# From the second write into the feed-forward: where the first units, the sums and the drain stand in each engine's queue

## The chip, the cores and the metric

The kernel runs on one core of one Trainium2 chip. The metric is the device time of one execution in microseconds; lower is better. The five engines of the core take their instructions in program order, each from its own queue, and wait for each other on semaphores. They are called PE (TensorE, matmuls), DVE (VectorE), ACT (ScalarE), POOL (GpSimd) and SP (SyncE, which issues the DMAs here).

## The reference, cut to what matters

The input x has 2 x 1024 rows of 2048 values. A block of attention and MLP is added to it, and then a feed-forward with quantised weights. The second write ends the first part, the feed-forward is the second:

```python
        out = o_d[..., :H]                       # y @ wod.T, and the low part of the deltas
        delta = jax.nn.softplus(delta_low @ du_w.T + du_b)
        A_neg = -jax.nn.softplus(A_logit)
        A_bar = jnp.exp(delta * A_neg)
        B_bar = (A_bar - 1.0) / (A_neg - SSM_EPS) * B_proj
        return (hs * A_full + out * B_full).reshape(b, l, H * C)
...
    x = x + _L0_xattn_ref(_layernorm(x, axis=-1), ...)
    x = x + _L0_ffn_ref(_layernorm(x, axis=-1), ...)   # w = (q - zp) * scale; out = x @ w.T + bias
```

## The kernel before

The last part of the program is one block (`build_middle`) in which `w1`, `mlp`, `w2` and `ffn` follow each other on every engine. The two that matter are the second write, `w2`, and the feed-forward, `ffn`. There are 16 tiles of 128 rows (`TILES`).

**The second write.** `steps` runs a software pipeline. In step s, tile s is loaded and split (`live(0)`), the products of tile s - 1 run on PE (`live(1)`, L1731: 48 triples of products, float32 done as high and low parts), tile s - 2 gets its gates, softplus and deltas (`live(2)`), tile s - 3 is updated and stored to the tensor x3 (`live(3)`, `res`), tile s - 4 is normalised and turned on PE (L1763), and tile s - 5 is stored turned, to xnT. The last five or six steps (s = 16 to 21) only empty the pipeline. After each of them `steps` calls `after(s - 16)`, and that is where the feed-forward puts its first work ahead: `sync_ahead`, `tensor_ahead`, `scalar_ahead`, `vector_ahead`. In step 17 (tile 15 in `live(2)`, nothing in `live(1)`) PE does `turn_small` (L1742) and `deltas` (L1748); ACT needs the first for `dlT` (L1871) and the second for the softplus (L1831 to L1837), which DVE's gates (L1976 to L1982) and POOL's gains (L1918 to L1926) wait for.

**The feed-forward.** 64 units: the 2048 outputs are four planes of 512 (c = u // 16), each over the 16 tiles. A unit is 16 x 3 matmuls of 128x512 (L2492 to L2494) into one of two banks `psF`. Its rows come from xnT into `xl` (`load_x`, three buffers, 1 MB), ACT copies the high part to `xh` (`hi_x`, L2383, two buffers), and DVE subtracts it to leave the low part (`lo_x`, L2387). The sum x3 comes into `xb` (`load_base`, two buffers, 256 KB), POOL adds the bias (L2475), DVE adds the bank (`finish`, L2448), SP stores it to y. The weights of plane 0 lie ready in the tensor wF: eight pairs are loaded (`load_first`, 512 KB each) and split by ACT (L2392) and DVE (L2397). Those of plane c + 1 are made during tiles 4 to 11 of plane c, two pieces to a unit (`made_in`): SP loads them (`load_piece`, 256 KB each, and every second unit two tiles of scales and zeros, `sz`, whose access repeats each of 8 rows 16 times), DVE subtracts the zeros (`less_zero`, L2416), POOL multiplies (L2421), ACT copies the high part (L2404), DVE leaves the low part (L2409).

What sets the order is the text itself. DVE's queue for unit u is

```python
                for v in made_in(u):
                    less_zero(dve, v)
                finish(dve, u)
                if u + 2 < UNITS:
                    lo_x(dve, u + 2)
                for v in made_in(u):
                    lo_piece(dve, v)
```

PE's unit u waits for `x_lo` of its own rows and `y_ok` of unit u - 2. `load_x(u)` waits until the buffer is free, `mm_ok >= u - 2`, which is the end of unit u - 3; the four first ones wait for the turned tile's store as well.

## Time and profile before

| | us |
|---|---|
| median of three runs | 2422.25 (2421.19 to 2428.3) |
| the profiled execution | 2416.85 |
| its span, first to last instruction | 2415.1 |
| PE busy in the span | 2188.6 (91%) |
| PE's weight loads | 1794.0 (74%) |
| DVE, ACT, POOL busy | 1329.1 (55%), 1068.7 (44%), 982.2 (41%) |

Times in the profile are us from the start of the span, of one execution. A row of a timeline gives start, duration, engine, line and operation with what it writes and reads, and in brackets how long its engine stood idle before it and what released it. The span lies 1.75 us under the execution's own time, and that 5.4 us under the median. The last matmul of the second write ends at 1637.1; the feed-forward's 64 units start between 1657.3 and the end.

### The profile page before, as it was taken

How to read it: one execution, taken by the hardware profiler on the slowest of the kernel's cores; microseconds unless marked ns; L12 is line 12 of the kernel's file. 1: busy time of each engine (PE TensorE's matmuls, PEld its weight loads, DVE VectorE, ACT ScalarE, POOL GpSimd, SP SyncE). 2: the span in 40 equal slices, each digit the busy share in tenths (PEclk: the TensorE clock that was granted, in tenths of full speed). 3: DMA queues.
4: the chain of work that ended last, by engine and by line, in shares of the span. 5: the costliest groups of instructions: out<-in, count | busy, mean ns of one | idle time of the engine just before them, and what ended most of it. 6: DMA issues, size and time to landing. Idle time of an engine off the chain costs nothing.

```text
span 2415.1 us, 34037 instructions
## 1 busy us (share of the span) xinstructions
PE 2188.6 (91%) x11560; PEld 1794.0 (74%) x11560; DVE 1329.1 (55%) x1744; ACT 1068.7 (44%) x1595; POOL 982.2 (41%) x613
## 2 busy tenths in 40 slices
PE   4898958999994999799999999995599999999999
PEld 2777745666663888688788889994478888888887
DVE  4777745777754899423332267675256265265222
ACT  2445425888882788621322356654222122122111
POOL 0111115999994777300000287762144144154110
PEclk8899987999996999899999999997799999999999
DMA  3678741333324666445454567866365465465443
GB/s 130 199 246 247 241 142 58 101 98 101 98 63 153 209 239 240 163 135 170 153 156 147 182 260 296 306 250 252 121 218 192 140 200 192 159 198 192 139 149 96
DMA packets 208614, 424.61 MB, mean 176 GB/s; under 512 B 16434, under 2 KB 131890, under 8 KB 181636
## 3 DMA queue, kind: packets, MB, share of 16 engines
q1 hardware_dynamic: 208516, 423.31, 53.3%
q8 instruction: 61, 1.00, 0.2%
q14 instruction: 37, 0.30, 0.0%
HBM read 284.31 MB, written 138.67 MB: 175 GB/s over the span
## 4 chain that ended last, share of the span: by engine, by line
PE 57%; DVE 4%; ACT 3%; DMA 2%; issue 2%; POOL 1%; SPq 0%; DVEq 0%; ACTq 0%; POOLq 0%
PE s_psF L2492 10%; PE s_psF L2493 10%; PE s_psF L2494 10%; PE s_m_psG L2141 7%; PE s_m_psU L2141 7%; PE s_w_psA L1731 4%; PE s_w_psB L1731 4%; PE s_w_psT L1763 1%; DVE s_w_ab L1511 1%; PE s_w_psB L1202 1%; DMA s_f_xl<-xnT 1%; PE s_w_psR L1250 1%; PE s_w_psT L1748 1%; PE s_w_psA L1212 1%; PE s_w_psT L1233 0%
## 5 line engine op out<-in xcount | busy, mean ns | idle before, releaser
L2492 PE MATMUL s_psF<-s_f_wh,s_f_xh 128*128 128x512 f32 x1024 | 402.7, 393 | 52.6 <-DVE s_f_xl L2387 32.3
L2494 PE MATMUL s_psF<-s_f_wh,s_f_xl 128*128 128x512 f32 x1024 | 401.3, 392 | 0.0
L967 POOL TENSOR_TENSOR s_a_pl<-s_a_pf,s_a_ph 128x1024 fp32r<-128x1024 f32 x128 | 302.0, 2391 | 22.2 <-ACT s_a_pf L932 22.1
L2383 ACT ACTIVATE s_f_xh<-s_f_xl 128x2048 fp32r<-128x2048 f32 x64 | 122.8, 1918 | 391.7 <-PE s_psF L2494 347.6
L2492 PEld LDWEIGHTS s_psF<-s_f_wh,s_f_xh 128*128 128x128 f32 x1024 | 194.4, 190 | 94.3 <-DVE s_f_xl L2387 33.1
L877 DVE TENSOR_REDUCE s_a_mx<-s_psS 128x1 f32<-128x512 f32 (+7 forms) x256 | 185.0, 754 | 119.5 <-PE s_psS L807 119.1
L2475 POOL TENSOR_TENSOR s_f_xb<-s_f_xb,s_f_fb 128x512 f32<-128x512 f32 x64 | 94.2, 1473 | 353.1 <-DMA s_f_xb<-x 353.1
L1895 POOL TENSOR_TENSOR s_w_yl<-s_w_y,s_w_yh 128x1024 fp32r<-128x1024 f32 x32 | 76.1, 2404 | 372.1 <-ACT s_w_yh L1809 372.1
L2494 PEld LDWEIGHTS s_psF<-s_f_wh,s_f_xl 128*128 128x128 f32 x1024 | 194.3, 190 | 40.7
L2493 PE MATMUL s_psF<-s_f_wl,s_f_xh 128*128 128x512 f32 x512 | 202.4, 395 | 0.0
L2387 DVE TENSOR_TENSOR s_f_xl<-s_f_xl,s_f_xh 128x2048 fp32r<-128x2048 f32 x64 | 160.9, 2514 | 71.5 <-ACT s_f_xh L2383 71.5
L2448 DVE TENSOR_TENSOR s_f_xb<-s_psF,s_f_xb 128x512 f32<-128x512 f32 x64 | 44.0, 687 | 250.7 <-PE s_psF L2494 218.1
L929 ACT ACTIVATE s_a_ph<-s_psX 128x1024 fp32r<-128x1024 f32 (+1 forms) x160 | 150.8, 942 | 57.0 <-PE s_psX L833 53.3
L2421 POOL TENSOR_TENSOR s_f_q<-s_f_q,s_f_sz 128x512 f32<-128x512 f32 x48 | 116.0, 2436 | 140.0 <-DVE s_f_q L2416 140.0
L458 POOL TENSOR_TENSOR s_q_qk<-s_q_ra,s_q_rb 128x1024 f32<-128x1024 f32 x16 | 37.7, 2359 | 294.8 <-DVE s_q_rb L690 294.8
L799 PE MATMUL s_psS<-s_a_k,s_a_q 96*128 96x512 f32 (+3 forms) x384 | 124.4, 413 | 35.4 <-DVE s_a_mx L877 19.7
L2493 PE MATMUL s_psF<-s_f_wl1a,s_f_xh 128*128 128x512 f32 x384 | 149.4, 389 | 0.0
L2201 DVE TENSOR_TENSOR s_m_mo<-s_m_psU,s_m_sil 128x512 f32<-128x512 f32 x64 | 44.2, 690 | 176.9 <-PE s_m_psU L2141 109.3
L851 PE MATMUL s_psO<-s_a_ph,s_a_vs 128*65 128x512 f32 (+3 forms) x384 | 128.5, 351 | 7.4 <-POOL s_a_pl L967 7.4
L932 ACT ACTIVATE s_a_pf<-s_psX 128x1024 f32<-128x1024 f32 x128 | 131.0, 1024 | 0.0
L851 PE MATMUL s_psO<-s_a_pl,s_a_vs 128*65 128x512 f32 (+3 forms) x384 | 125.3, 338 | 0.0
L2493 PEld LDWEIGHTS s_psF<-s_f_wl,s_f_xh 128*128 128x128 f32 x512 | 98.4, 192 | 20.5
(311 smaller groups left out, 5583.6 us busy)
## 6 DMA issues: line engine op xcount, KB each, us to landing
s_f_xl<-xnT SPq DMA_DIRECT2D x64, 1024.0 KB, 5.6
s_q_xt<-xT SPq DMA_DIRECT2D x16, 1024.0 KB, 7.7
s_q_xc<-xP SPq DMA_DIRECT2D x16, 1024.0 KB, 9.7
hsD<-s_q_hs SPq DMA_DIRECT2D x16, 1024.0 KB, 4.9
s_w_hin<-hsD SPq DMA_DIRECT2D x16, 1024.0 KB, 4.9
hs<-s_w_res SPq DMA_DIRECT2D x16, 1024.0 KB, 3.9
s_m_raw<-giT SPq DMA_DIRECT2D x32, 512.0 KB, 4.6
mlpT<-s_m_mo SPq DMA_DIRECT2D x64, 256.0 KB, 2.4
```

The lines of the kernel that those rows point to most:

```text
L799: pe.matmul(psS[:, at:at + n], qa[0:K3, p, qi * P:(qi + 1) * P], ka[0:K3, p, kk:kk + n], start=True, stop=not last)
L851: mm = pe.matmul(psO[0:VW, half, 512 - n:512], vs[:, r, ki, :], part[:, r, at:at + n], start=(ki == 0 and part is ph), stop=(ki == (3, 7)[ ...
L877: dve.tensor_reduce(mx[:, slot % 2, qi:qi + 1], psS[:, off:off + (qi + 1) * P], AX, ALU.max).then_inc(mx_ok, 1)
L929: act.activation(ph[:, r, at:at + wide[j]], src, ACT.Exp, scale=scale).then_inc(exp_ok, 1)
L932: act.activation(full, src, ACT.Exp, scale=scale).then_inc(exp_ok, 1)
L967: pool.tensor_tensor(pl[:, r, cols], pf[:, j - 1], ph[:, r, cols], ALU.subtract).then_inc(pl_ok, 1)
L1731: mm = pe.matmul(bank[:, 0:n], a[:, p, kt], b[:, kt, cols], start=False, stop=(kt == KM - 1 and a is yl))
L2141: mm = pe.matmul(bank[u % 2][:], a[:, kt], b[:, :, kt], start=(i == 0 and a is w[m][0] and b is xh), stop=(i == KH - 1 and a is w[m][1]))
L2387: dve.tensor_tensor(xl[u % 3][:], xl[u % 3][:].bitcast(F32), xh[:, u % 2], ALU.subtract).then_inc(x_lo, 1)
L2492: pe.matmul(out[:], xh[:, u % 2, kt], high(c, kt), start=(kt == 0), stop=False)
L2493: pe.matmul(out[:], xh[:, u % 2, kt], low(c, kt), start=False, stop=False)
L2494: mm = pe.matmul(out[:], xl[u % 3][:, kt], high(c, kt), start=False, stop=(kt == KD - 1))
```

## The change

Nothing is computed differently; instructions and DMAs move within the queues, and with them the waits.

- PE: units 0 and 1 move from behind step 16 into step 17 (`amid`), behind `turn_small` and `deltas`.
- ACT: behind step 16 only `hi_x(0)` remains. The eight copies of the first weights, `hi_x(1)` and `hi_x(2)` move into step 17, behind `dlT` and ahead of the softplus. `hi_x(3)` and `hi_x(4)` follow steps 17 and 18.
- DVE: `finish(0)` and `lo_x(2)` stand in step 17 behind the gates, ahead of the statistics; `finish(1)`, `lo_x(3)` behind step 17, `finish(2)`, `lo_x(4)` behind step 18.
- POOL: the first two sums are copied (with the bias) behind steps 16 and 17.
- SP: tile 0's rows are loaded behind step 16 once the products of tile 14 are done; the rest follows step 17. `serve(u)` (store of y, load of the sum u + 2, load of the rows u + 4) runs for units 0 to 2 between the last steps, the wait for all of the write's stores (`drained`) only then, and `serve` for units 3 to 63 in the loop. Before, the loop loaded the rows u + 3, ahead of the sum.

```diff
         def sync_ahead(sp, i):
             if i == 0:
+                sp.wait_ge(w2["ab_mm"], 2 * (TILES - 1))
+                load_x(sp, 0)
+            if i == 1:
                 sp.wait_ge(w2["ab_mm"], 2 * TILES)
-                load_x(sp, 0)
                 for pair in range(PAIRS):
                     load_first(sp, pair)
                 load_x(sp, 1)
-            if i == 1:
+                load_base(sp, 0)
                 sp.dma_start(fb[:], io["fbias"]).then_inc(fb_in, 16)
-                load_base(sp, 0)
                 load_base(sp, 1)
                 load_x(sp, 2)
-            if i == 2:
                 load_x(sp, 3)
+            if 2 <= i < 5:
+                serve(sp, i - 2)
+
+        def serve(sp, u):
+
+            c, tile = u // TILES, u % TILES
+            sp.wait_ge(y_ok, u + 1)
+            sp.dma_start(io["y"][tile * P:(tile + 1) * P, c * H:(c + 1) * H], xb[:, u % 2]).then_inc(y_out[u % 2], 16)
+            if u + 2 < UNITS:
+                load_base(sp, u + 2)
+            if u + 4 < UNITS:
+                load_x(sp, u + 4)
 
         def sync(sp):
-            for u in range(UNITS):
+            w2["drained"](sp)
+            for u in range(3, UNITS):
                 c, tile = u // TILES, u % TILES
                 if FROM <= tile < FROM + PAIRS and c + 1 < C:
                     for v in range(2):
                         load_piece(sp, (c + 1) * KD + 2 * (tile - FROM) + v)
-                sp.wait_ge(y_ok, u + 1)
-                sp.dma_start(io["y"][tile * P:(tile + 1) * P, c * H:(c + 1) * H], xb[:, u % 2]).then_inc(y_out[u % 2], 16)
-                if u and u + 3 < UNITS:
-                    load_x(sp, u + 3)
-                if u + 2 < UNITS:
-                    load_base(sp, u + 2)
+                serve(sp, u)
...
         def scalar_ahead(act, i):
             if i == 0:
                 hi_x(act, 0)
-                for pair in range(PAIRS):
-                    hi_first(act, pair)
-            if i < 3:
-                hi_x(act, i + 1)
+            elif i < 3:
+                hi_x(act, i + 2)
+
+        def scalar_amid(act):
+            for pair in range(PAIRS):
+                hi_first(act, pair)
+            hi_x(act, 1)
+            hi_x(act, 2)
...
+        def vector_amid(dve):
+            finish(dve, 0)
+            lo_x(dve, 2)
...
+        def gpsimd_ahead(pool, i):
+            if i == 0:
+                pool.wait_ge(fb_in, 16)
+            if i < 2:
+                with_bias(pool, i)
...
+        def tensor_amid(pe):
+            unit(pe, 0)
+            unit(pe, 1)
+
         def tensor_ahead(pe, i):
-            if i == 0:
-                unit(pe, 0)
-            if i < 3:
+            if 1 <= i < 3:
                 unit(pe, i + 1)
```

First place, ACT's queue at the end of step 16, where the first rows (`xh`), the first weights (`wh`), the write's last sums (`pa`), the low deltas (`dlT`) and the softplus (`sp`) stand. Before:

```order
L2383 ACTIVATE s_f_xh<-s_f_xl_4814 128x2048
L2392 ACTIVATE s_f_wh_4810<-s_f_wl_4811 128x1024 x8
L2383 ACTIVATE s_f_xh<-s_f_xl_4815 128x2048
L1821 ACTIVATE s_w_pa<-s_w_psA 128x312
L1823 ACTIVATE s_w_pa<-s_w_psB 128x320
L1871 ACTIVATE s_w_dlT<-s_w_psT 9x128
L1831 ACTIVATE s_w_sp<-s_w_psT 128x512
```

After:

```order
L2399 ACTIVATE s_f_xh<-s_f_xl_4814 128x2048
L1825 ACTIVATE s_w_pa<-s_w_psA 128x312
L1827 ACTIVATE s_w_pa<-s_w_psB 128x320
L1875 ACTIVATE s_w_dlT<-s_w_psT 9x128
L2408 ACTIVATE s_f_wh_4810<-s_f_wl_4811 128x1024 x8
L2399 ACTIVATE s_f_xh<-s_f_xl_4815 128x2048
L2399 ACTIVATE s_f_xh<-s_f_xl_4812 128x2048
L1835 ACTIVATE s_w_sp<-s_w_psT 128x512
```

The copy of the sums and of the low deltas moved ahead of the weights, and the rows of unit 2 ahead of the softplus.

Second place, SP's queue at units 4 and 5 of a plane (`y` is the output's store, `xl` the rows, `xb` the sum, `sz` scales and zeros, `q` the pieces). Before:

```order
L2371 DMA y<-s_f_xb 128x512
L2339 DMA s_f_xl_4814<-xnT 128x2048
L2347 DMA s_f_xb<-x 128x512
L2328 DMA s_f_sz<-scT 128x1x512
L2328 DMA s_f_sz<-zpT 128x1x512
L2331 DMA s_f_q<-wq 128x512 x2
L2371 DMA y<-s_f_xb 128x512
L2339 DMA s_f_xl_4815<-xnT 128x2048
L2347 DMA s_f_xb<-x 128x512
L2331 DMA s_f_q<-wq 128x512 x2
```

After:

```order
L2378 DMA y<-s_f_xb 128x512
L2355 DMA s_f_xb<-x 128x512
L2347 DMA s_f_xl_4815<-xnT 128x2048
L2336 DMA s_f_sz<-scT 128x1x512
L2336 DMA s_f_sz<-zpT 128x1x512
L2339 DMA s_f_q<-wq 128x512 x2
L2378 DMA y<-s_f_xb 128x512
L2355 DMA s_f_xb<-x 128x512
L2347 DMA s_f_xl_4812<-xnT 128x2048
L2339 DMA s_f_q<-wq 128x512 x2
```

The rows' load moved behind the sum's and is that of the next unit's buffer (4815 in place of 4814): it stands directly ahead of the pieces.

## Rows read from the trace of the kernel before

**Rows 1.** Timeline of PE, handover: start us, us, engine line op, idle before
```profile
1657.33 0.77 PE L2492 MATMUL s_psF<-s_f_wh,s_f_xh 128*128 128x512 f32 x1 [20.22 <-ACT s_w_pa L1823]
...
1687.72 3.67 PE L1763 MATMUL s_w_psT<-c_ident,s_w_xn 128*128 128x128 f32 x16 [5.30 <-ACT s_w_xn L1852]
...
1698.78 0.80 PE L2492 MATMUL s_psF<-s_f_wh,s_f_xh 128*128 128x512 f32 x1 [7.39 <-DVE s_f_xl L2387]
...
1712.60 1.03 PE L1763 MATMUL s_w_psT<-c_ident,s_w_xn 128*128 128x128 f32 x8
...
1719.84 0.80 PE L2492 MATMUL s_psF<-s_f_wh,s_f_xh 128*128 128x512 f32 x1 [4.81 <-DVE s_f_xl L2387]
...
1755.98 0.79 PE L2492 MATMUL s_psF<-s_f_wh,s_f_xh 128*128 128x512 f32 x1 [20.12 <-DVE s_f_xl L2387]
...
1768.61 0.39 PE L2492 MATMUL s_psF<-s_f_wh,s_f_xh 128*128 128x512 f32 x1
```
**Rows 2.** Timeline of SP, handover: weight pairs issued, first output stored
```profile
1637.53 4.12 SPq L2318 DMA_DIRECT2D s_f_wl<-wF  x8
...
1740.44 0.33 SPq L2371 DMA_DIRECT2D y<-s_f_xb  x1
```
**Rows 3.** Timeline of ACT, handover
```profile
1647.08 1.06 ACT L2392 ACTIVATE s_f_wh<-s_f_wl 128x1024 fp32r<-128x1024 f32 x1 [0.23 <-DMA s_f_wl<-wF]
...
1652.18 1.06 ACT L2392 ACTIVATE s_f_wh<-s_f_wl 128x1024 fp32r<-128x1024 f32 x1 [0.21 <-DMA s_f_wl<-wF]
1654.67 1.91 ACT L2383 ACTIVATE s_f_xh<-s_f_xl 128x2048 fp32r<-128x2048 f32 x1 [1.43 <-DMA s_f_xl<-xnT]
...
1682.46 0.60 ACT L1831 ACTIVATE s_w_sp<-s_w_psT 128x512 f32<-128x512 f32 x1 [1.21 <-PE s_w_psT L1748]
...
1768.87 1.92 ACT L2383 ACTIVATE s_f_xh<-s_f_xl 128x2048 fp32r<-128x2048 f32 x1 [11.20 <-PE s_psF L2494]
```
**Rows 4.** Timeline of DVE, handover
```profile
1646.12 9.17 DVE L2397 TENSOR_TENSOR s_f_wl<-s_f_wl,s_f_wh 128x1024 fp32r<-128x1024 f32 x8
...
1658.82 2.29 DVE L1946 TENSOR_TENSOR s_w_psAB<-s_w_psAB,s_w_t 128x2048 f32<-128x2048 f32 x1
...
1684.79 0.70 DVE L1976 SCALAR_TENSOR_TENSOR s_w_psAB<-s_w_psT,s_w_sp 128x512 f32<-128x512 f32 x1 [18.95 <-ACT s_w_sp L1837]
...
1685.98 1.74 DVE L1982 TENSOR_TENSOR s_w_psAB<-s_w_psAB,s_w_gate 128x1536 f32<-128x1536 f32 x1
```
**Rows 5.** Timeline of SP, plane 1: row loads with and without scales behind them
```profile
1956.76 0.43 SPq L2339 DMA_DIRECT2D s_f_xl<-xnT  x1
...
1969.78 0.43 SPq L2339 DMA_DIRECT2D s_f_xl<-xnT  x1
```
**Rows 6.** Timeline of DVE: two plain finishes, then pieces, finish and split
```profile
1877.61 0.69 DVE L2448 TENSOR_TENSOR s_f_xb<-s_psF,s_f_xb 128x512 f32<-128x512 f32 x1 [6.58 <-PE s_psF L2494]
...
1888.48 0.69 DVE L2448 TENSOR_TENSOR s_f_xb<-s_psF,s_f_xb 128x512 f32<-128x512 f32 x1 [6.58 <-PE s_psF L2494]
...
1967.44 1.32 DVE L2416 TENSOR_TENSOR s_f_q<-s_f_q,s_f_sz 128x512 f32<-128x512 int32 x2 [5.00 <-DMA s_f_q<-wq]
...
1969.28 2.78 DVE L2387 TENSOR_TENSOR s_f_xl<-s_f_xl,s_f_xh 128x2048 fp32r<-128x2048 f32 x1
...
1977.22 1.32 DVE L2416 TENSOR_TENSOR s_f_q<-s_f_q,s_f_sz 128x512 f32<-128x512 int32 x2 [1.77 <-DMA s_f_q<-wq]
```
**Rows 7.** View of the tile of rows (xl): its 64 loads
```profile
DMA to landing us min/median/max: 4.8/5.6/23.6
```
**Rows 8.** Timeline of PE in the MLP, behind a wait of 3.90 us
```profile
1178.09 0.50 PE L2141 MATMUL s_m_psG<-s_m_xhXB,s_m_wh 128*128 128x512 f32 x1 [3.90 <-ACT s_m_sil L2100]
...
1178.89 0.39 PE L2141 MATMUL s_m_psG<-s_m_xhXB,s_m_wh 128*128 128x512 f32 x1
1179.12 0.59 PE L2141 MATMUL s_m_psG<-s_m_xlXB,s_m_wh 128*128 128x512 f32 x1
...
1182.07 0.63 PE L2141 MATMUL s_m_psG<-s_m_xhXB,s_m_wl 128*128 128x512 f32 x1
```

More of the change, by code:

```diff
@@ L1716, in sync, with drained @@
             steps(sp, TILES, LAST + 1, 2, body, LAST + 2, start=1, after=after)
+        def drained(sp):
             sp.wait_ge(t_out, 16 * TILES)
@@ L1719, in sync, with tensor @@
                 sp.wait_ge(out, 16 * TILES // len(st_out))
-        def tensor(pe, after):
+        def tensor(pe, after, amid):
             pe.wait_ge(prep, 4)
@@ L1786, in body @@
                         deltas(s)
+                        if not live(1):
+                            amid()
                     if kt == 12 and live(4):
@@ L1809, in hi_y, with scalar @@
             act.activation(yh[:, p, part], yraw[:, part], ACT.Copy).then_inc(y_hi, 1)
-        def scalar(act, after):
+        def scalar(act, after, amid):
             act.add_instruction(mybir.InstLoadActFuncSet(
@@ L1871, in body @@
                     act.activation(dlT[:], psT[0][0:S0, 0:P], ACT.Copy).then_inc(dl_ok, 1)
+                    if not live(1):
+                        amid()
                 if live(0):
@@ L1887, in scalar, with gpsimd @@
             steps(act, TILES, LAST, 2, body, LAST + 1, start=1, after=after)
-        def gpsimd(pool):
+        def gpsimd(pool, after):
             def lo_y(s, p, half):
@@ L1935, in body, with vector @@
                     gains(s, p)
-            steps(pool, TILES, LAST, 2, body, LAST + 1)
-        def vector(dve, after):
+            steps(pool, TILES, LAST, 2, body, LAST + 1, after=after)
+        def vector(dve, after, amid):
             dve.wait_ge(mlp["mm_u"], CHUNKS * KM)
@@ L1989, in body @@
                     gates(s, p)
+                    if not live(1):
+                        amid()
                 if live(3):
@@ L1997, in build_write2 @@
                     hi_y=lambda act, half: hi_y(act, first, 0, half),
-                    ab_mm=ab_mm, pa_ok=pa_ok, d_mm=d_mm, t_out=t_out, st_out=st_out)
+                    ab_mm=ab_mm, pa_ok=pa_ok, t_out=t_out, st_out=st_out, drained=drained)
 def build_mlp(nc, io, k, zone, w1, plane):
@@ L2432, in scalar_ahead @@
                 hi_x(act, 0)
-                for pair in range(PAIRS):
-                    hi_first(act, pair)
-            if i < 3:
-                hi_x(act, i + 1)
+            elif i < 3:
[5 more added lines that the diff above has]
+            hi_x(act, 2)
         def scalar(act):
-            for u in range(2, UNITS):
+            for u in range(3, UNITS):
                 if u + 2 < UNITS:
@@ L2454, in vector_ahead @@
                     lo_first(dve, pair)
+                lo_x(dve, 1)
             elif i < 3:
-                finish(dve, i - 1)
-            if i < 3:
-                lo_x(dve, i + 1)
+                finish(dve, i)
+                lo_x(dve, i + 2)
+        def vector_amid(dve):
+            finish(dve, 0)
+            lo_x(dve, 2)
         def vector(dve):
-            for u in range(2, UNITS):
+            for u in range(3, UNITS):
                 for v in made_in(u):
@@ L2468, in vector, with with_bias @@
                     lo_piece(dve, v)
-        def gpsimd(pool):
-            pool.wait_ge(fb_in, 16)
-            for u in range(UNITS):
-                c = u // TILES
-                pool.wait_ge(xb_in[u % 2], 16 * (u // 2 + 1))
-                pool.tensor_tensor(xb[:, u % 2], xb[:, u % 2], fb[:, c * H:(c + 1) * H], ALU.add).then_inc(b_ok, 1)
+        def with_bias(pool, u):
+            c = u // TILES
+            pool.wait_ge(xb_in[u % 2], 16 * (u // 2 + 1))
+            pool.tensor_tensor(xb[:, u % 2], xb[:, u % 2], fb[:, c * H:(c + 1) * H], ALU.add).then_inc(b_ok, 1)
+        def gpsimd_ahead(pool, i):
[3 more added lines that the diff above has]
+                with_bias(pool, i)
+        def gpsimd(pool):
+            for u in range(2, UNITS):
+                with_bias(pool, u)
                 for v in made_in(u):
@@ L2507, in build_ffn @@
         return dict(sync=sync, tensor=tensor, scalar=scalar, gpsimd=gpsimd, vector=vector, sync_ahead=sync_ahead,
-                    tensor_ahead=tensor_ahead, scalar_ahead=scalar_ahead, vector_ahead=vector_ahead)
+                    tensor_ahead=tensor_ahead, scalar_ahead=scalar_ahead, vector_ahead=vector_ahead, gpsimd_ahead=gpsimd_ahead,
+                    tensor_amid=tensor_amid, scalar_amid=scalar_amid, vector_amid=vector_amid)
 def build_middle(nc, io, k):
@@ L2537, in _ @@
             mlp["tensor"](pe)
-            w2["tensor"](pe, lambda i: ffn["tensor_ahead"](pe, i))
+            w2["tensor"](pe, lambda i: ffn["tensor_ahead"](pe, i), lambda: ffn["tensor_amid"](pe))
             ffn["tensor"](pe)
@@ L2550, in _ @@
             w1["gpsimd"](pool, lambda i: mlp["gpsimd_ahead"](pool, i))
-            w2["gpsimd"](pool)
+            w2["gpsimd"](pool, lambda i: ffn["gpsimd_ahead"](pool, i))
             ffn["gpsimd"](pool)
```

5 lines of the change are left out of this document (2 added, 3 removed).

## The prediction

> **What bounds the kernel now.** I read first the timeline of TensorE (PE) where the change acts, then, for each wait in it, the timeline of the engine named as its releaser, and then the same for the later units. The feed-forward is 64 units of 48 matmuls, one unit every 10.88 us when nothing holds PE [rows 6]. Between the last product of the second write (it ends at 1637.1) and the start of unit 4 (1755.98), PE has only four units and some turns to do in 118.9 us. It waits 20.22, 5.30, 7.39, 4.81 and 20.12 us there, 57.8 in all [rows 1]. The causes differ. The first rows and weights are loaded and split only now. ScalarE's (ACT's) softplus waits for a small product that stands behind units 0 and 1 on PE. SyncE (SP) stores no output and reloads no sum before the write has drained: the first store is at 1740.44 [rows 2]. After a long wait the clock is low for a while as well: unit 2 takes 13.82 us (1698.78 to 1712.60) instead of 10.88 [rows 1].
>
> The later 60 units end one every 10.88 us. In 24 of them (tiles 4 to 11 of three planes) VectorE (DVE) dequantises two pieces of the next plane before it finishes the unit. DVE waits there for the pieces' DMA, 5.00 us before 1967.44 [rows 6], but PE waits for nothing.
>
> **First part: the handover.** I follow it from 1637.1.
> - Unit 0. The eight weight pairs are issued at 1637.5 as before [rows 2], since the last products still gate them; ahead of them in the queue is a tile's store in place of a tile's load, 1 MB either way. They land one each 1.27 us: the fourth is copied at 1647.08, the eighth at 1652.18 [rows 3], which puts the first near 1643.3. With 1.06 for ACT's copy and 1.15 for DVE's [rows 3, 4], PE starts near 1645.6, not at 1657.33, and works behind the arriving pairs. 10.88 and 1.7 for a cold start (unit 4 took 12.63, 1755.98 to 1768.61 [rows 1]) end it at 1658.2.
> - The last tile's copy of its sums, its small turn and its delta product now come ahead of this, between 1638.5 and 1641, when all three engines would stand waiting for the loads. They cost nothing.
> - Unit 1 needs tile 1's rows: landed at 1654.67, split by 1658.8 [rows 3, 4]. It ends near 1669.7.
> - Unit 2: its rows land after 2.5 MB more, near 1661 at a pair's rate (512 KB in 1.27 us). ACT copies them (1.9) and only then runs softplus. From its start to DVE's gates are 2.3 us (1682.46 to 1684.79 [rows 3, 4]), so 1665.3; DVE's update of 7.0 us (from 1658.82 to 18.95 before 1684.79 [rows 4]) ends at 1665.9. Gates 2.9 (1684.79 to 1687.72 [rows 4]), one sum 0.69, one split 2.78 [rows 6]: unit 2 starts at 1672.3, when PE has just done the turn. The waits of 5.30 and 7.39 are gone.
> - Units 2 and 3, and turns of 2.43 us (1712.60 to 1715.03 [rows 1]): 1683.2, 1685.6, 1696.5, and unit 4 starts at 1698.9. Its rows are loaded between the units and wait for no drain.
>
> Unit 4 now starts at 1755.98 and runs some 1.7 us cold. So 1755.98 + 1.7 - 1698.9 = 58.8 [rows 1]; I take **58.5 us gained**, 50 to 61 (several chains end within a microsecond of each other, and a late row load shifts them). The waits say the same: 57.8 and about 10 of low clock go, about 9 of new waits and one cold start stay.
>
> **Second part: what the new queue of SP does to the later units.** The row load moves from `load_x(u + 3)` to `load_x(u + 4)`, and it waits for unit u + 1, which runs at that time; before it waited for unit u, which was done. So SP stands still until unit u + 1 ends. Behind it stand the pieces of step u + 1 (the order of SP, second place), and DVE dequantises these *before* it finishes unit u + 1. They were loaded during the unit; now they are issued at its end. I count from e, when DVE could finish unit u.
> - The row load is issued at e + 0.1. Alone it lands in 4.8 us at best [rows 7].
> - *A step with scales* (every second one, 12 in all) loads two scale tiles and two pieces behind the rows. The trace doesn't show this with nothing between. It shows 10.68 us from row load to DVE's first piece (1956.76 to 1967.44 [rows 5, 6]), with a sum of 256 KB between, 0.65 us at a pair's rate. Of that 4.8 + 0.65 are rows and sum, so 5.2 are scales and pieces: 4.8 + 5.2 = 10.0. It can't be worse than 11.0, as now, nor better than 7.3 (1 MB more at a pair's rate). I take 10.0, nearest to a row.
> - From DVE's first piece to the end of the next split are 4.62 us (1967.44 to 1972.06 [rows 6]): PE gets unit u + 2 at e + 14.77. It would be free for it at e + 10.62 (10.88 less 0.26 from PE's 1768.61 to ACT's 1768.87 [rows 1, 3]). **PE waits 4.15 us**, 12 times.
> - *A step without scales*: 7.44 (1969.78 to 1977.22 [rows 5, 6]) less 0.65, with the 4.7 on top e + 11.5: late by 0.9 at most. A cold unit in between absorbs it.
> - The clock: after a wait of 3.90 us PE soon ran 8 matmuls at 0.43 us apart, not 0.23, which lost 1.6 us [rows 8]; after 7.39 it lost 2.9. I take 1.6, the nearer row.
>
> 12 x (4.15 + 1.6) = 69, and 1.3 because SP comes late to unit 4 from the drain: **70.3 us lost**. Before, DVE's first piece could come 6.0 us after e unnoticed (10.62 - 4.62); this spends it.
>
> The Trainium skill (DMA: Bandwidth & Descriptors, Rules for kernel authors) wants a DMA issued early and waited for late; for the pieces this change does the reverse. The same section says that an outermost dimension below 16 confines a DMA to that many engines, and a scale tile's is 8. By that rule the scales take twice the time of their bytes behind the rows too, and the pieces come near 10; without it they would come nearer to 8 and the change would gain. The trace agrees: the 0.5 MB of scales makes 10.68 of 7.44 us [rows 5, 6], 3.2 us against 1.27 for a weight pair.
>
> **Small edits.** The sums' copies on GpSimd, the base loaded ahead of the bias, the later drain: nothing waits for them within 5 us.
>
> **Sum.** The profiled execution takes 2416.85, 5.4 less than the median of the three runs. 2416.85 - 58.5 + 70.3 = 2428.7; from the median, 2422.25 + 11.8 = **2434**.
>
> **Rivals.**
> 1. *The clock holds* through waits of 4 us. 12 x (4.15 + 0.7) + 1.3 = 59.5: 2423, no change. Against it: [rows 8].
> 2. *The pieces come sooner*, 8.9 after the row load, with nothing between: the wait is 3.05 and the clock mostly holds. 12 x 3.1 + 1.3 = 38.5: **2402, faster**. Any cost under 4.8 us a pair of units (57.2 / 12) makes the change a gain.
> 3. *No new wait*: the pieces lie in time, or SP isn't held. 2422 - 58 = 2364. SP's order speaks against it.
> 4. *Both at their worst*: 11.0 and 2.9. 12 x (5.15 + 2.9) + 1.3 = 98: 2462.
> 5. *The handover brings less than it says*: row loads late, PE waiting twice more, 40 gained. 2422 - 40 + 70 = 2452.
>
> **How the numbers follow.** Forecast 0.43; rivals 0.24, 0.17, 0.05, 0.06, 0.05. No change is within 0.3% (7 us), about what a measurement of this kernel can tell. Faster: rivals 2 and 3 and a fifth of rival 1, 0.27. Same: the rest of rival 1 and the forecast's low edge, 0.26. Slower: 0.47. The range, 2400 to 2453, leaves out rivals 3 and 4 and the ends of 2 and 5.
>
> **What would show it.** Right: unit 4 starts near 1699; SP issues pieces just after a unit's end; DVE idles about 9 us ahead of them in a step with scales; PE idles 12 times about 4 us until a split of rows ends, with a granted clock of one half behind it (1.2 of 2.4 GHz). Wrong: waits below 3 us, a clock that holds, or PE without a break from unit 4 on.

## The result: slower by 0.6%, the gain of the handover more than spent

| | before | after |
|---|---|---|
| median, us | 2421.72 (4 runs, 2417.8 to 2428.3) | 2437.09 (4 runs, 2433.02 to 2439.18) |
| profiled execution | 2416.85 | 2436.12 |
| its span | 2415.1 | 2434.4 |
| from the last product group of the second write to the end of the span | 779.2 | 795.4 |

The ratio of after to before is 1.0057, with a 95% interval from 1.0039 to 1.0076. The forecast was 2434, in a range from 2400 to 2453. The last row of the table leaves out what the earlier stages, which the change doesn't touch, take in one execution or another. It is the span less the last start in these two groups (the view of one line of the program; columns: duration in ns min/median/max, first to last start in us), before and then after:

```profile
L1731 PE MATMUL s_w_psA<-s_w_wh,s_w_yl x256: 302/307/310, 1359.8 to 1635.9; 128*128 128x312 f32 x128
```
```profile
L1733 PE MATMUL s_w_psA<-s_w_wh,s_w_yl x256: 302/307/312, 1363.2 to 1639.0; 128*128 128x312 f32 x128
```

So 16.2 us of the 19.3 between the two profiled executions come from the changed part. I call this quantity the *tail* and use it for every run below. It comes from one execution of each kernel and so has no interval.

**The handover after the change.** Timeline of PE; it answers [rows 1]:

```profile
1639.87 0.30 PE L1733 MATMUL s_w_psB<-s_w_wh,s_w_yl 128*128 128x320 f32 x1
...
1649.17 0.77 PE L2524 MATMUL s_psF<-s_f_wh,s_f_xh 128*128 128x512 f32 x1 [5.25 <-DVE s_f_wl L2413]
...
1673.47 1.03 PE L1765 MATMUL s_w_psT<-c_ident,s_w_xn 128*128 128x128 f32 x8
...
1702.35 0.47 PE L2524 MATMUL s_psF<-s_f_wh,s_f_xh 128*128 128x512 f32 x1
```

The last product ends at 1640.17. Unit 0 starts 9.0 us later (before: 20.2), and unit 4 starts at 1702.35, 62.2 us later, where it took 118.9 and a cold start of 1.7. The waits of 20.22, 5.30, 7.39, 4.81 and 20.12 [rows 1] are one of 5.25 now and a few under 1.8. The handover gained 118.9 + 1.7 - 62.2 = 58.4 us.

**The later units.** From unit 4 to the end of the span are 2434.4 - 1702.35 = 732.0 us; before they were 2415.1 - 1755.98 - 1.7 = 657.4. So 74.6 were lost, 16.2 net. The waits view of PE from 1715 on (columns: waiter and releaser, us in total, times, longest) has one row for them. In the kernel before, the same view has only the handover's waits of 4.81 and 20.12 there, and none behind unit 4:

```profile
PE s_psF L2524 <- DVE s_f_xl L2403: 50.7, 12, 9.0
```

Most of the other 23.9 us go with the low clock behind these waits. Of the twelve units that follow them, ten take 12.4 to 13.8 us instead of 10.88, and two, behind waits of 3.07 and 3.55 us, 11.0 and 11.3; that is 21.4 us in all. The rest lies in the units just ahead of the waits. The costliest of the twelve (13.8 us) in the timeline of PE, in plane 1:

```profile
1958.16 0.79 PE L2524 MATMUL s_psF<-s_f_wh,s_f_xh 128*128 128x512 f32 x1 [4.09 <-DVE s_f_xl L2403]
1958.75 0.63 PE L2525 MATMUL s_psF<-s_f_wl1a,s_f_xh 128*128 128x512 f32 x1
...
1963.87 0.51 PE L2525 MATMUL s_psF<-s_f_wl1a,s_f_xh 128*128 128x512 f32 x1
```

After 4.09 us without work, 13 matmuls follow each other at 0.43 us instead of 0.23 (the first starts at 1958.16, the second at 1958.75, the fourteenth at 1963.87), at the lower of the clock's two levels, 1.2 GHz (the granted clock from 1958.16 to 1963.90 is 0.50). Why it waits is seen on the two engines ahead of it. The timeline of SP, one step without scales and the next with them:

```profile
1958.14 0.43 SPq L2347 DMA_DIRECT2D s_f_xl<-xnT  x1
...
1966.33 0.34 SPq L2378 DMA_DIRECT2D y<-s_f_xb  x1
1968.63 0.33 SPq L2355 DMA_DIRECT2D s_f_xb<-x  x1
1972.14 0.33 SPq L2347 DMA_DIRECT2D s_f_xl<-xnT  x1
1972.51 0.63 SPq L2336 DMA_DIRECT2D s_f_sz<-scT  x1
...
1973.83 1.10 SPq L2339 DMA_DIRECT2D s_f_q<-wq  x2
```

and of DVE, the same pieces:

```profile
1964.38 1.32 DVE L2432 TENSOR_TENSOR s_f_q<-s_f_q,s_f_sz 128x512 f32<-128x512 int32 x2 [2.90 <-DMA s_f_q<-wq]
...
1981.81 1.32 DVE L2432 TENSOR_TENSOR s_f_q<-s_f_q,s_f_sz 128x512 f32<-128x512 int32 x2 [9.41 <-DMA s_f_q<-wq]
```

SP issues the sum at 1968.63, stands 3.2 us, and sends the rows at 1972.14, when the running unit ends. The pieces are issued behind them, and DVE has the first one 9.67 us after the row load (9.23 to 11.09 in the twelve steps with scales, 9.93 in the mean; the forecast took 10.0), having idled 9.41 us. This is the picture that the prediction drew. But SP stands at the row load for 1.8 us in the mean of the twelve steps, and in five of them for less than 0.4: there the load of the sum, which waits until the store of y has *landed* (is written in memory), has held SP until the unit's end or past it. The experiments show that this is a second cause, and that each of the two is enough.

### The profile page after: what moved, and what is told of

The parts are those of the page before. It is cut to its first block, busy times and chain, and to the rows that moved or that the text cites. A ratio compares the mean times of both kernels' runs of the same rounds, so it can differ in the third digit from the quotient of the medians.

```text
span 2434.4 us, 34037 instructions
## 1 busy us (share of the span) xinstructions
PE 2209.0 (91%) x11560; PEld 1805.0 (74%) x11560; DVE 1332.9 (55%) x1744; ACT 1065.2 (44%) x1595; POOL 987.4 (41%) x613
## 4 chain that ended last, share of the span: by engine, by line
PE 48%; DMA 8%; DVE 5%; ACT 3%; issue 2%; POOL 1%; SPq 1%; DVEq 0%; ACTq 0%; POOLq 0%
PE s_psF L2524 7%; PE s_psF L2526 7%; PE s_psF L2525 7%; PE s_m_psG L2149 7%; PE s_m_psU L2149 7%; DMA s_f_q<-wq 5%; PE s_w_psA L1733 4%; PE s_w_psB L1733 4%; DMA y<-s_f_xb 1%; PE s_w_psT L1765 1%; PE s_w_psR L1250 1%; DVE s_w_ab L1511 1%; DVE s_f_xl L2403 1%; PE s_w_psB L1202 1%; POOL s_f_q L2437 1%
## 5 line engine op out<-in xcount | busy, mean ns | idle before, releaser
L2524 PE MATMUL s_psF<-s_f_wh,s_f_xh 128*128 128x512 f32 x1024 | 410.4, 401 | 56.1 <-DVE s_f_xl L2403 50.7
L967 POOL TENSOR_TENSOR s_a_pl<-s_a_pf,s_a_ph 128x1024 fp32r<-128x1024 f32 x128 | 302.0, 2393 | 21.9 <-ACT s_a_pf L932 21.8
L2420 ACT ACTIVATE s_f_wh<-s_f_q 128x512 fp32r<-128x512 f32 x48 | 30.3, 632 | 256.2 <-POOL s_f_q L2437 256.2
```

The source lines that it names most:

```text
L967: pool.tensor_tensor(pl[:, r, cols], pf[:, j - 1], ph[:, r, cols], ALU.subtract).then_inc(pl_ok, 1)
L2524: pe.matmul(out[:], xh[:, u % 2, kt], high(c, kt), start=(kt == 0), stop=False)
```

## Experiments

Theory A is the prediction's: SP stands at the row load until the running unit ends, and the pieces behind it come late. Its first rival, B, is that the transfers themselves or the new start-up order make them late. More rivals came up with the runs and are named in what was expected of each.

Each is given with its ratio to the kernel before from the same chip and that ratio's 95% interval. The kernel before took medians of 2420.0 to 2426.4 us in the four sets. Set beside the kernel before, tail and ratio agree within about 3 us in most runs, but are 5 apart in e7, 7 in e4 and 9 in e2. Differences of a few us between two tails are therefore not clear of noise.

| run | median | ratio, interval | tail | less |
|---|---|---|---|---|
| after | 2437.1 | 1.0057 (1.0039 to 1.0076) | 795.4 | before: +16.2 |
| e1_pieces_ahead | 2369.4 | 0.9793 (0.9771 to 0.9815) | 727.9 | before: -51.3 |
| e2_loop_order_alone | 2490.7 | 1.0299 (1.0261 to 1.0338) | 842.8 | before: +63.6 |
| e3_rows_near | 2428.3 | 1.0024 (1.0004 to 1.0044) | 785.2 | e1: +57.3 |
| e4_units_ahead_of_product | 2392.1 | 0.9897 (0.9860 to 0.9933) | 747.1 | e1: +19.2 |
| e5_scales_ahead | 2421.0 | 0.9993 (0.9980 to 1.0006) | 777.1 | after: -18.3 |
| e6_scales_16_engines | 2403.6 | 0.9920 (0.9893 to 0.9947) | 762.3 | after: -33.1 |
| e7_matmuls_in_waits | 2426.8 | 1.0010 (0.9995 to 1.0024) | 786.8 | after: -8.6 |
| e8_plain_pieces_behind | 2390.5 | 0.9871 (0.9842 to 0.9901) | 749.8 | e1: +21.9 |
| e9_sum_first_no_stand | 2463.9 | 1.0185 (1.0160 to 1.0211) | 821.1 | before: +41.9 |
| e10_rows_ahead_of_sum | 2445.6 | 1.0102 (1.0078 to 1.0125) | 803.4 | after: +8.0 |
| e11_pieces_ahead_16 | 2372.2 | 0.9794 (0.9772 to 0.9815) | 726.3 | e1: -1.6 |
| e12_pieces_ahead_of_sum | 2368.4 | 0.9768 (0.9749 to 0.9788) | 723.1 | e1: -4.8 |

### The two halves of the change, apart

**e1_pieces_ahead**: the changed kernel with the pieces ahead of the row load, so that the handover is left without the late pieces.

```diff
             if u + 2 < UNITS:
                 load_base(sp, u + 2)
+            for v in made_in(u + 1):
+                load_piece(sp, v)
             if u + 4 < UNITS:
                 load_x(sp, u + 4)
...
             for u in range(3, UNITS):
-                c, tile = u // TILES, u % TILES
-                if FROM <= tile < FROM + PAIRS and c + 1 < C:
-                    for v in range(2):
-                        load_piece(sp, (c + 1) * KD + 2 * (tile - FROM) + v)
                 serve(sp, u)
```

> The changed kernel; SyncE issues the pieces of step u+1 after the sum of unit u+2 and ahead of the row load that waits for unit u+1. Nothing else differs. Theory A (SyncE's standing at the row load is what makes the pieces late, and the waits and the low clock behind them are the whole loss of the later units): the 12 waits of TensorE for the split of rows go (50.7 us in all, with some 24 us of low clock), the gain of the handover stays: 2437 - 74 = 2363, at most 2368. Rival B (the pieces are late because their transfers now share the queues with other loads, or because of the new start-up order of the engines, wherever SyncE issues them): waits of over 2 us stay in most of the 12 steps and the time is 2415 to 2437.

**e2_loop_order_alone**: the loop alone, in the kernel before.

```diff
-                if u and u + 3 < UNITS:
-                    load_x(sp, u + 3)
                 if u + 2 < UNITS:
                     load_base(sp, u + 2)
+                if u + 4 < UNITS:
+                    load_x(sp, u + 4)
```

> The kernel before with only SyncE's loop over the units changed: first the sum of unit u+2, then the rows of unit u+4, which wait for unit u+1. The handover stays as before. Theory A: 12 waits of 3.5 to 4 us with some 2 us of low clock behind each, 65 to 75 us lost: 2487 to 2497, and unit 4 starts near 1756 as before. Rival B (the loss needs the new handover): 2422, no change.

The handover without the late pieces takes 51.3 us off the tail, and the loop's order alone adds 63.6 (2369.4 us, just over the 2368 that theory A allowed, and 2490.7, inside its range). e2 holds both edits of the loop, the sum ahead of the rows and the rows of u + 4 for those of u + 3, and doesn't tell them apart. Rival B (other transfers, or the new start-up order) is out, since the loss is there without the new handover and gone with it. In e1 one wait of rows was left in the whole feed-forward, besides one of 0.53 us; timeline of PE:

```profile
1742.29 0.80 PE L2522 MATMUL s_psF<-s_f_wh,s_f_xh 128*128 128x512 f32 x1 [4.66 <-DVE s_f_xl L2401]
```

With some 2 us of clock behind it, this is why 51.3 came and not 58.

### Is it SP's standing at the row load?

**e3_rows_near**: the changed kernel, where the loop's row load is one that waits for nothing.

```diff
             if u + 2 < UNITS:
                 load_base(sp, u + 2)
-            if u + 4 < UNITS:
-                load_x(sp, u + 4)
+            if u and u + 3 < UNITS:
+                load_x(sp, u + 3)
```

> The changed kernel with the row load of the loop put back to unit u+3 (it waits for unit u, which is done, and so never holds SyncE); it still stands ahead of the pieces, behind the sum, and the handover stays as changed. Theory A: no wait stands ahead of the pieces, so they arrive as in the kernel before: 2363, the same as with the pieces ahead of the row load, within 5 us. Rival C (what counts is that 1 MB of rows goes through the DMA engines ahead of the pieces, not that SyncE waits): the pieces still come some 10 us behind the row load, but the row load now starts some 10 us earlier, so by this rival also waits of 1 to 4 us would remain if other transfers push in: 2375 to 2437.

Theory A said 2363 and the run took 2428.3, so A fails as a full account. First, part of it is a side effect of the edit: rows 4 now come a store later, ACT stands 15.5 us for them in the handover, PE waits 10.20 us for the turn behind, and unit 4 starts 75.3 us after the last product group, where it was 63.4. The rest is not: PE waits for the split of rows 14 times, 34.8 us in all. Timeline of SP, two steps (with scales, without):

```profile
1781.98 1.33 SPq L2347 DMA_DIRECT2D s_f_xl<-xnT  x1
...
1794.54 0.34 SPq L2378 DMA_DIRECT2D y<-s_f_xb  x1
1796.92 0.33 SPq L2355 DMA_DIRECT2D s_f_xb<-x  x1
1797.35 0.38 SPq L2347 DMA_DIRECT2D s_f_xl<-xnT  x1
...
1806.43 0.34 SPq L2378 DMA_DIRECT2D y<-s_f_xb  x1
1808.81 0.33 SPq L2355 DMA_DIRECT2D s_f_xb<-x  x1
1809.24 0.38 SPq L2347 DMA_DIRECT2D s_f_xl<-xnT  x1
```

and the pieces on DVE:

```profile
1792.62 1.29 DVE L2432 TENSOR_TENSOR s_f_q<-s_f_q,s_f_sz 128x512 f32<-128x512 int32 x2 [7.37 <-DMA s_f_q<-wq]
...
1804.51 1.29 DVE L2432 TENSOR_TENSOR s_f_q<-s_f_q,s_f_sz 128x512 f32<-128x512 int32 x2 [3.91 <-DMA s_f_q<-wq]
```

This is a closed chain. The store of y can't go before DVE has finished the unit, and DVE finishes it behind the pieces. The sum's load waits until the store has landed (1794.54 to 1796.92, 2.4 us), and the rows and the pieces stand behind it. One round of two units is 10.64 (rows to the first piece) + 1.92 (to the store) + 2.81 (to the next rows) + 7.16 + 1.92 + 2.81 = 27.26 us; PE needs 21.76 for them. Rival C (the rows' 1 MB ahead of the pieces is what counts) foretold the time, but not this reason: the kernel before has the rows ahead of the pieces too, 11.1 us ahead in the mean against 10.5 here, and PE doesn't wait. In the kernel before, the rows went *ahead* of the sum, so that their transfer ran while the store landed. Its stores in the same place, in the timeline of SP, are 23.19 us apart (one round; between the other row loads of such steps it is 22.8 to 24.4):

```profile
1780.40 0.34 SPq L2371 DMA_DIRECT2D y<-s_f_xb  x1
...
1803.59 0.34 SPq L2371 DMA_DIRECT2D y<-s_f_xb  x1
```

That is 1.43 over PE's 21.76, four times in a plane, 5.7 us, which just fits into the 6.0 us that the prediction had found free. That is worked out, not tried. I call the chain theory F and tried it alone.

**e9_sum_first_no_stand**: the kernel before with one swap, in which no load waits for a running unit.

```diff
-                if u and u + 3 < UNITS:
-                    load_x(sp, u + 3)
                 if u + 2 < UNITS:
                     load_base(sp, u + 2)
+                if u and u + 3 < UNITS:
+                    load_x(sp, u + 3)
```

> The kernel before with one swap in SyncE's loop: the sum of unit u+2, which waits until the store of unit u has landed, goes ahead of the rows of unit u+3, which wait for nothing. No load here waits for a unit that runs. Theory A as predicted (only SyncE's standing at the row load costs): 2424, no change. Theory F (a closed chain: store of y, its landing 2.4 us, rows, pieces, dequantising, finish, next store; with the rows behind the landing it takes some 26.6 us for a pair of units, as in e3_rows_near, where TensorE needs 21.76): 12 pairs, less the slack of some 5 us in each plane, as e3_rows_near lost it against e1_pieces_ahead apart from its handover: some 47 more, 2460 to 2475.

**e10_rows_ahead_of_sum**: the changed kernel with the reverse swap, so that only the stand is left.

```diff
-            if u + 2 < UNITS:
-                load_base(sp, u + 2)
             if u + 4 < UNITS:
                 load_x(sp, u + 4)
+            if u + 2 < UNITS:
+                load_base(sp, u + 2)
```

> The changed kernel with the row load, which waits for unit u+1, ahead of the sum of unit u+2: SyncE stands at the rows while the store lands, so the landing costs nothing of its own, and the sum's 256 KB stand ahead of the pieces. Theory A (the stand alone is enough): pieces 10.7 us behind the rows in a step with scales, so PE's wait is 4.8 with 2 us of low clock: 28.6 us for a pair of units, 2437 to 2450. Theory F alone (only the landing ahead of the rows costs): the chain is as in the kernel before, 23 us for a pair: some 2375.

e9 took 2463.9, where A said 2424: the swap alone costs 41.9 us of tail (1.6 of them ahead of unit 4). A round of it, 26.66 us; timeline of PE:

```profile
1998.84 0.50 PE L2492 MATMUL s_psF<-s_f_wh,s_f_xh 128*128 128x512 f32 x1 [2.61 <-DVE s_f_xl L2387]
...
2025.50 0.50 PE L2492 MATMUL s_psF<-s_f_wh,s_f_xh 128*128 128x512 f32 x1 [2.99 <-DVE s_f_xl L2387]
```

e10 took 2445.6, where F alone said 2375: the stand alone is enough too. In its timeline of SP the store and the rows are 7.0 us apart, with nothing between, and the pieces' first use (2014.30) is 11.05 us behind the rows, about the 11.0 that the prediction had as the worst (10.34 to 11.15 in the twelve steps):

```profile
1996.21 0.34 SPq L2378 DMA_DIRECT2D y<-s_f_xb  x1
2003.25 0.33 SPq L2347 DMA_DIRECT2D s_f_xl<-xnT  x1
```

Its waits view of PE from 1715 on has twelve waits again:

```profile
PE s_psF L2524 <- DVE s_f_xl L2403: 54.8, 12, 4.9
```

The sum's 256 KB between rows and pieces don't explain it: the kernel before has them there as well. So there are two chains, and either one is enough: a round of two units takes 28.7 us in the mean in e10, 27.8 in the changed kernel and about 26.6 in e9 once its rounds have settled, against 21.76. They don't add, since the stand at the rows overlaps the landing of the store: the changed kernel has both, e10 only the stand and e9 only the landing.

### Which steps, and what lies ahead of the pieces

**e8_plain_pieces_behind**: e1, but the twelve steps without scales as in the changed kernel (the edit is given against the changed kernel).

```diff
+            for v in made_in(u + 1):
+                if u % 2:
+                    load_piece(sp, v)
             if u + 4 < UNITS:
...
-                    for v in range(2):
+                    for v in range(2 * (tile % 2)):
```

> As e1_pieces_ahead in the steps with scales, and as the changed kernel in the 12 steps without them (their pieces behind the row load that waits). Theory A as predicted: steps without scales are late by at most 0.9 us and cost nothing much: 2369 to 2381. Rival E (every step in which SyncE waits ahead of the pieces costs alike, the scales matter little): half of the 68 us comes back, 2403.

It cost 21.9 us of tail against e1 (by the ratios 19), 1.6 to 1.8 us a step where the prediction had at most 0.9. With 2390.5 us it lies between theory A (2369 to 2381) and rival E (2403), and neither fits. The waits view of PE from 1715 on:

```profile
PE s_psF L2527 <- DVE s_f_xl L2406: 20.3, 11, 6.8
```

In the changed kernel the steps without scales show no wait of their own. PE comes to them late and at the low clock, which is the likely reason: in e7 below, where the clock mostly stays up, waits of 0.7 to 1.5 us stand ahead of six such units. The steps with scales carry the larger part: the changed kernel's tail is 67.5 us over e1's in all.

**e5_scales_ahead**: the changed kernel with the two scale tiles ahead of the row load (`load_scales` is that part of `load_piece`, taken out of it).

```diff
...
                 load_base(sp, u + 2)
+            for v in made_in(u + 1):
+                if v % 4 == 0:
+                    load_scales(sp, v)
             if u + 4 < UNITS:
                 load_x(sp, u + 4)
```

> The changed kernel; only the two scale tiles of step u+1 are issued ahead of the row load that waits for unit u+1, the two pieces stay behind it. Theory A: the steps with scales now look like those without: some 7.2 us from the row load to DVE's first piece instead of 10.7 (both are intervals that traces show), so the waits of 3 to 5 us shrink to 1 us or less, at a clock that mostly holds: 12 x 5.8 less, plus up to 1 us in each of the 24 steps: 2369 to 2393. Rival D (bytes count, not their place: the scales were hidden anyway and the wait comes from the pieces' own landing): 2430 to 2437.

It gave 18.3 us of tail, less than half of the 44 to 68 that A said. DVE has its first piece 8.34 us behind the rows in the mean of the twelve steps (5.67 to 9.68), 1.6 sooner than in the changed kernel and not the 7.2 that was expected. The scales go out only when the store has landed, a few us ahead of the rows, and the time from the first scale tile to the first piece is not shorter but longer, 10.4 us in the mean against 9.6. Timeline of SP in the step with 9.68 (first piece at 1998.80), where the scales are 2.7 us ahead:

```profile
1986.05 0.33 SPq L2357 DMA_DIRECT2D s_f_xb<-x  x1
1986.43 0.63 SPq L2341 DMA_DIRECT2D s_f_sz<-scT  x1
...
1989.12 0.33 SPq L2349 DMA_DIRECT2D s_f_xl<-xnT  x1
```

**e6_scales_16_engines**: the same bytes into the same tile, but each partition's row read as a row.

```diff
-                    sp.dma_start(sz[:, r, side], spread(io[name][v // 4].unsqueeze(1), GR, P // GR, H)).then_inc(sz_in[r], 16)
+                    sp.dma_start(sz[:, r, side], io[name + "P"][v // 4]).then_inc(sz_in[r], 16)
...
+        "scTP": np.repeat(groups(a["sc"]), 16, axis=1),
+        "zpTP": np.repeat(groups(a["zp"]), 16, axis=1),
```

> The changed kernel, with each scale tile read from an array in memory that has a row for each of the 128 partitions, instead of 8 rows that are spread over 16 partitions each. Bytes written and places are the same. If the form of the old load confines it to 8 of 16 DMA engines (the Trainium skill's rule, DMA: Bandwidth & Descriptors, Rules for kernel authors), 0.5 MB of scales costs about 1.3 us (a weight pair's rate) instead of 3.2: the 12 waits shrink by some 1.9 us each and the clock gives a little back, 23 to 30 us in all: 2407 to 2414. If the form doesn't matter: 2437.

33.1 us less tail; the time of 2403.6 lies a little below the forecast of 2407 to 2414. Timeline of SP; DVE's first piece is at 1988.57, 8.11 us behind the rows:

```profile
1980.46 0.33 SPq L2347 DMA_DIRECT2D s_f_xl<-xnT  x1
1980.83 0.43 SPq L2336 DMA_DIRECT2D s_f_sz<-scTP  x1
```

In the twelve steps it is 7.94 us in the mean (6.87 to 9.17) against 9.93, so 2.0 us a step, as expected (1.9); 0.4 of it because the two issues take 0.43 us each instead of 0.63 and 0.60. The Trainium skill (DMA: Bandwidth & Descriptors, Rules for kernel authors) says that an outermost dimension below 16 confines a DMA to at most that many engines, and here it is 8. The trace agrees. The view of stretches (columns: the stretch, its us, busy time and count of PE, PEld, DVE, ACT and POOL, PEclk, DMA share, GB/s) over the last transfers ahead of the first piece, when the rows have landed, first of the changed kernel, then of e6:

```profile
1979.14:1981.14 2.00, 2.00 (x10) 1.65 (x10) 0.00 (x0) 0.00 (x0) 0.00 (x0) 1.00 0.52 177
```
```profile
1986.20:1987.40 1.20, 1.20 (x7) 1.01 (x6) 0.00 (x0) 0.00 (x0) 0.00 (x0) 1.00 0.97 362
```

The 16 DMA engines are half busy in the mean with the old form and fully busy with the new one, at twice the rate. Which engine a load used isn't in the trace, and the new form also reads 128 rows of memory instead of 8 many times, which no run takes apart. So the rule is well supported but not shown.

**e7_matmuls_in_waits**: work added, to keep TensorE's clock.

```diff
-        _, *psF = banks(nc, "s6_", ("psAB", [P, C, 512]), ("psF0", [P, H]), ("psF1", [P, H]))
+        spare, *psF = banks(nc, "s6_", ("psAB", [P, C, 512]), ("psF0", [P, H]), ("psF1", [P, H]))
...
             c, tile = u // TILES, u % TILES
+            if made_in(u - 2) and tile % 2 == 0:
+                for kt in range(14):
+                    pe.matmul(spare[:, 0], high(c, kt)[:, 0:P], high(c, kt), start=True, stop=True)
             pe.wait_ge(x_lo, u + 1)
```

> The changed kernel with 14 more matmuls into an unused bank at the start of every unit that follows a step with scales, which is where TensorE waits 3 to 5 us; their result is used nowhere. At 0.23 us each they fill 3.2 us of the wait and end before it does. If the low clock behind the waits costs what the trace of the changed kernel says (some 24 us over 12 waits), the time falls to 2413 to 2420 although work is added. If the clock isn't part of the loss: 2437 or more.

The clock did stay up, but for the unit behind the first wait (13.6 us). The view of stretches from 1900 to 2100, first of the changed kernel, then of this one:

```profile
1900.00:2100.00 200.00, 185.69 (x781) 151.27 (x780) 87.01 (x64) 40.11 (x32) 64.16 (x32) 0.96 0.51 158
```
```profile
1900.00:2100.00 200.00, 196.28 (x857) 159.94 (x856) 89.43 (x65) 40.32 (x33) 63.93 (x32) 1.00 0.53 165
```

The granted clock is 1.00 instead of 0.96. But only 8.6 us of tail came back (by the ratios 11), not 17 to 24. The 14 matmuls are 38 us over twelve waits, and PE still idles 18.7 us for rows: 57 us where it was 50.7. The units end sooner, and SP's stand at the row load is 0.3 us or less in nine of the twelve steps with scales (in four of the changed kernel). But the load of the sum goes out no sooner for it, since the store behind which it waits follows the pieces on DVE; what is left is mostly the round of e9, which doesn't pass through PE. So "wait plus clock" adds up for the time that was lost, but not for what a repair of the clock alone would give back.

### What makes up the gain of the handover

**e4_units_ahead_of_product**: e1 with units 0 and 1, the first weights' copies and rows 1 back ahead of the last small product (the same lines are gone from `tensor_amid` and `scalar_amid`).

```diff
-            if 1 <= i < 3:
+            if i == 0:
+                unit(pe, 0)
+                unit(pe, 1)
+            elif i < 3:
                 unit(pe, i + 1)
...
                 hi_x(act, 0)
+                for pair in range(PAIRS):
+                    hi_first(act, pair)
+                hi_x(act, 1)
```

> As e1_pieces_ahead, but TensorE runs units 0 and 1, and ScalarE copies the first weights and rows 1, ahead of the last tile's small product, as in the kernel before; loads, drain and the rest stay as changed. Theory A: the last softplus and DVE's gates start only when unit 1 ends, so TensorE waits some 8 to 9 us for the split of rows 2 where it waits 0.3 now, with 2 us of low clock: 8 to 13 us more than e1_pieces_ahead, some 2374. If the order of the small product carries most of the 58 us of the handover, it is 30 us or more instead; if DVE's other work hides it, it is 0 to 3.

It lost 19.2 us of tail against e1 (by the ratios 25), between the two cases. The expectation had seen one wait only. ACT's copy of the last tile's sums now stands behind the eight copies of weights and the copy of rows 1, and unit 0 stands with it, since `unit` waits for that copy (`pe.wait_ge(w2["pa_ok"], 2 * TILES)` for units 0 and 1); then comes the wait for the turn. Timelines of ACT and of PE:

```profile
1665.10 0.43 ACT L1827 ACTIVATE s_w_pa<-s_w_psB 128x320 f32<-128x320 f32 x1
```
```profile
1665.63 0.76 PE L2522 MATMUL s_psF<-s_f_wh,s_f_xh 128*128 128x512 f32 x1 [20.15 <-ACT s_w_pa L1827]
...
1696.36 3.42 PE L1765 MATMUL s_w_psT<-c_ident,s_w_xn 128*128 128x128 f32 x16 [5.75 <-ACT s_w_xn L1856]
```

These are 20.15 and 5.75, as 20.22 and 5.30 in [rows 1]. The place of the copy and of the small product is a third or somewhat more of the handover's 58 us. The rest, earlier rows and the later drain, was not taken apart.

### A version that beats both

**e11_pieces_ahead_16**: e1 with the scale tiles of e6 (both edits are above).

> e1_pieces_ahead with the scale tiles of e6_scales_16_engines: both changes that paid. In e1_pieces_ahead TensorE still waits 4.66 us once (the first step with scales, to which SyncE comes late from the handover) and some 2 us of low clock follow; less DMA time ahead of the pieces takes away most of that: 2362 to 2367, against 2369. If the transfers were hidden there anyway: 2369.

**e12_pieces_ahead_of_sum**: e1 with the pieces ahead of the sum as well.

```diff
+            for v in made_in(u + 1):
+                load_piece(sp, v)
             if u + 2 < UNITS:
                 load_base(sp, u + 2)
-            for v in made_in(u + 1):
-                load_piece(sp, v)
             if u + 4 < UNITS:
```

> e1_pieces_ahead with the pieces of step u+1 ahead of the sum of unit u+2 too, so that they wait neither for the running unit nor for the landing of the store; rows last, as there. In e1_pieces_ahead the first step with scales is issued at 1730.67, 6.2 us after the store at 1724.12, since that store lands late behind the handover's 1 MB stores, and TensorE waits 4.66 us for it. Theory: the pieces now go out at 1724.6, the wait and some 2 us of low clock go, nothing waits after unit 4: 2360 to 2365, against 2369 for e1_pieces_ahead. If that first wait is caused by the DMA engines being busy and not by SyncE's stand, the pieces land no earlier: 2369.

e11 is e1 within the measurement: once no row load stands ahead of the pieces, the form of the scales is hidden. It missed its 2362 to 2367. In e12 the pieces go out right behind the store, as the rows below show, and the one long wait is 2.43 us, not 4.66; the median of 2368.4 can't be told from e1's 2369.4, and missed the 2365 that was expected at most. The tail is 4.8 us shorter. DVE still gets the first piece only at 1727.62, 10.5 us behind the first scale tile: there the DMA itself is late, behind 1 MB of rows at 1716.13. Timeline of SP:

```profile
1716.13 0.38 SPq L2347 DMA_DIRECT2D s_f_xl<-xnT  x1
1716.69 0.34 SPq L2378 DMA_DIRECT2D y<-s_f_xb  x1
1717.09 0.66 SPq L2336 DMA_DIRECT2D s_f_sz<-scT  x1
```

Both are 2.1 to 2.3% faster than the kernel before, and 2.6 to 2.9% faster than the changed one by the ratios.

## Why the prediction came out right, and what in it was wrong

- **The handover.** Forecast: unit 4 at 61.8 us after the last product, 58.5 gained. Measured: 62.2 and 58.4. Its chain (pairs, units 0 and 1 behind them, softplus ahead of the turn) held; unit 0 started 9.0 us after the last product, forecast 8.5.
- **The cause of the first wait.** The prediction put it down to the loads of rows and weights. In e4 they come as early as in e1, and the wait of 20.15 us is back: it is the order of ACT's copies. The change moved that too, so the sum held.
- **The waits of the later units.** Forecast 12 x 4.15 = 49.8 us; measured 50.7 in 12. The interval from rows to pieces was 9.93 in the mean (forecast 10.0). There was luck in it: the row that it was worked out from, 10.68, is a low one of twelve steps that took 10.47 to 11.70, 11.11 in the mean, which would have given 10.5 and some 5 us more in all. For the same reason "not worse than 11.0, as now" was too low a bound; the worst step took 11.09. (Its terms for PE's start add up to e + 14.72, not 14.77, which is 0.6 us over twelve steps.)
- **SP late from the drain.** This term was 1.3 us and was mis-sized: the first wait is 8.98, 4.8 over the others' forecast. The queue was held by two stores of y that landed late. The row load of that step went out at 1717.99, some 4.5 us after the unit that it waits for had ended; timeline of SP:

```profile
1703.32 0.34 SPq L1714 DMA_DIRECT2D xnT<-s_w_hT  x1
1703.72 0.42 SPq L2378 DMA_DIRECT2D y<-s_f_xb  x1
1710.26 0.34 SPq L2355 DMA_DIRECT2D s_f_xb<-x  x1
1710.69 0.38 SPq L2347 DMA_DIRECT2D s_f_xl<-xnT  x1
1711.26 0.34 SPq L2378 DMA_DIRECT2D y<-s_f_xb  x1
1717.58 0.33 SPq L2355 DMA_DIRECT2D s_f_xb<-x  x1
1717.99 0.38 SPq L2347 DMA_DIRECT2D s_f_xl<-xnT  x1
```

- **The other eleven waits** were 3.8 us in the mean, a little under the 4.15. That this and the first one's excess cancel is luck.
- **The clock.** 23.9 us for twelve waits, 2.0 each, where the forecast had 12 x 1.6 = 19.2 from the wait of 3.90 us [rows 8]. The unit behind a wait lost 0.2 to 2.9 us, and not by the wait's length: 2.9 behind 4.09 us, 2.2 behind 5.77, 0.2 behind 3.07. The second part lost 74.6 against 70.3; of the 4.3 between, the clock is 4.7, the waits 0.9, and the term of 1.3 for SP, which the waits contain, goes off.
- **The mechanism was half of it.** The step "it waits for unit u + 1 ... so SP stands still until unit u + 1 ends" is sufficient (e10), though in five of the twelve steps the landing hid the stand. But the prediction took the other edit in the same lines, the sum's load ahead of the rows, for free: it counted 0.65 us of transfer for it and not that this load waits 2.3 to 2.4 us for a store that itself waits for the pieces. Alone that costs 41.9 us (e9). That the number came out even so is luck: here the stand and the landing overlap, so the omitted one cost next to nothing. Had the change kept `load_x(u + 3)`, the prediction's reasoning would have given a gain of 58 us, and this would have been wrong by 64 (e3, with the side effect in its handover; 42 by e9's swap alone).
- **Steps without scales**, "late by 0.9 at most": in this kernel no wait shows; alone they cost 1.6 to 1.8 each (e8).
- **Rivals.** The clock held behind two of the twelve waits only (rival 1), and the pieces didn't come at 8.9 (rival 2). With the other form of the scales (e6) they came at 7.94 in the mean and the time was 2403.6, near rival 2's 2402, but by other waits: 17 of 29.1 us in all, where rival 2 had 12 of 3.05. Rival 3's 2364 is what e1 and e12 come near, 2369.4 and 2368.4.

## To carry to other kernels

In a queue that runs in order, a load that must wait belongs behind every load that need not, and the wait of each entry has to be looked up, also of small ones: here a 256 KB load whose wait was 2.4 us closed a chain through another engine. For each loop over several engines add up one full round (load, use, store, its landing, next load) and set it beside the time of the bounding engine; a round within some 7% of it, as 23.2 to 21.8 here, means that the next harmless edit becomes visible. A faster clock on an engine gives little back when such a round, which doesn't pass through it, sets the pace next (e7).
